# Four loads of w1 moved from SyncE's DMA queue to ScalarE's in a one-core decoder layer

## What is computed

```python
def _L0_attn_ref(x, w1, w2, b2, sparse_mask):
    attn = jnp.einsum('ds,td->st', w1, w2) * sparse_mask
    y = jnp.einsum('bds,st->bdt', x, attn) + b2
    return jax.nn.gelu(y, approximate=False)
...
x = _layernorm(x + _L0_attn_ref(x, L0_attn_w1, L0_attn_w2, L0_attn_b2, L0_attn_sparse_mask), axis=-1)
x = _layernorm(x + _L0_xattn_ref(x, ctx_4096, ctx_4096, mask_BxSxS2_ff0, ...), axis=-1)
x = _layernorm(x + _L0_ffn_ref(x, ...), axis=-1)
```

## Time and profile before

| | |
|---|---|
| median of 3 runs | 491.17 us |
| the profiled execution, its time | 490.72 us |
| its span, first to last instruction | 488.9 us |
| TensorE busy | 474.7 us (97%) |
| VectorE busy | 409.8 us (84%) |
| ScalarE busy | 269.2 us (55%) |
| GpSimd busy | 253.7 us (52%) |
| mean granted TensorE clock | 0.989 |

### The profile page before, as it was taken

One profiled execution on the slowest core, in us unless ns is written; L12 is line 12 of the kernel. 1 busy time (PEld: TensorE's weight loads), 2 busy tenths in 40 slices (PEclk: granted clock), 3 DMA queues, 4 the chain that ended last, 5 costly groups with the idle time before them and its releaser, 6 DMA issues.

```text
span 488.9 us, 11036 instructions
## 1 busy us (share of the span) xinstructions
PE 474.7 (97%) x4189; PEld 395.6 (81%) x4189; DVE 409.8 (84%) x733; ACT 269.2 (55%) x475; POOL 253.7 (52%) x250
## 2 busy tenths in 40 slices
PE   8999999999999999999999999999999999969994
PEld 8888778888888888888888888888888888757783
DVE  2779898988987898799879987998798989989666
ACT  4574447734673567356636673566357445574434
POOL 3377537863674477546746663677268421222300
PEclk9999999999999999999999999999999999979998
DMA  8942300230023002301130203021102300000004
GB/s 277 351 148 88 129 1 1 87 131 1 2 86 129 0 7 79 129 0 38 48 129 0 85 6 124 0 86 44 41 0 87 56 12 2 1 0 1 0 3 172
DMA packets 29137, 31.56 MB, mean 65 GB/s; under 512 B 6321, under 2 KB 16817, under 8 KB 29114
## 3 DMA queue, kind: packets, MB, share of 16 engines
q1 hardware_dynamic: 29114, 31.25, 19.5%
HBM read 29.15 MB, written 2.10 MB: 64 GB/s over the span
## 4 chain that ended last, share of the span: by engine, by line
PE 83%; DVE 12%; POOL 2%; ACT 1%; issue 1%; POOLq 0%; DVEq 0%; ACTq 0%
PE bank L262 24%; PE bank L264 23%; PE bank L263 23%; PE bank L370 7%; PE bank L394 3%; DVE VWl L1152 2%; DVE X L1252 1%; DVE BST L1200 1%; PE bank L283 1%; PE bank L268 1%; DVE X L1343 1%; DVE XTl L1152 1%; DVE QR L1186 1%; DVE bank L1280 1%; PE bank L427 0%
## 5 line engine op out<-in xcount | busy, mean ns | idle before, releaser
L1745 POOL TENSOR_TENSOR QS<-QS,SIN 128x512 f32<-128x512 f32 x64 | 82.9, 1295 | 132.3 <-ACT QS L802 132.3
L262 PE MATMUL bank<-XTh,WQh 128*128 128x512 f32 x256 | 102.0, 398 | 0.5 <-DVE XTl L1152 0.5
L264 PE MATMUL bank<-XTh,WQl 128*128 128x512 f32 x256 | 100.0, 391 | 0.0
L263 PE MATMUL bank<-XTl,WQh 128*128 128x512 f32 x256 | 99.7, 390 | 0.0
L1152 DVE TENSOR_TENSOR VWl<-bank,VWh 64x512 fp32r<-64x512 f32 x128 | 88.1, 688 | 9.7 <-ACT VWh L802 8.0
L802 ACT ACTIVATE QS<-bank 128x512 f32<-128x512 f32 x64 | 38.3, 598 | 96.9 <-PE bank L264 96.4
L802 ACT ACTIVATE VWh<-bank 64x512 fp32r<-64x512 f32 x128 | 75.7, 592 | 20.2 <-PE bank L264 17.5
L1280 DVE TENSOR_TENSOR bank<-bank,COS 128x512 f32<-128x512 f32 x64 | 44.6, 697 | 20.9 <-ACT QS L802 20.4
L262 PEld LDWEIGHTS bank<-XTh,WQh 128*128 128x128 f32 x256 | 48.1, 188 | 11.2 <-issue 1.2
L264 PEld LDWEIGHTS bank<-XTh,WQl 128*128 128x128 f32 x256 | 48.0, 188 | 10.5
L263 PEld LDWEIGHTS bank<-XTl,WQh 128*128 128x128 f32 x256 | 48.2, 188 | 9.4
(11 more groups left out here) (155 smaller groups left out, 954.5 us busy)
## 6 DMA issues: line engine op xcount, KB each, us to landing
WQr<-in_L_xattn_wq_dram SPq DMA_DIRECT2D x8, 1024.0 KB, 5.5
WOr<-in_L_xattn_wo_dram SPq DMA_DIRECT2D x8, 1024.0 KB, 5.1
KVr<-in_L_xattn_wk_dram SPq DMA_DIRECT2D x8, 256.0 KB, 5.1
KVr<-in_L_xattn_wv_dram SPq DMA_DIRECT2D x8, 256.0 KB, 5.4
out_dram<-X SPq DMA_DIRECT2D x8, 256.0 KB, 2.0
X<-in_x_dram SPq DMA_DIRECT2D x3, 512.0 KB, 10.1
WQr<-in_L_attn_w_dram SPq DMA_DIRECT2D x4, 256.0 KB, 5.1
WOr<-in_L_attn_w_dram SPq DMA_DIRECT2D x4, 256.0 KB, 5.3
```

Of the source, the lines that this page charges most:

```text
L262: pe.matmul(o, lh, rh, start=start, stop=False)
L263: pe.matmul(o, lh, rl, start=False, stop=False)
L264: return pe.matmul(o, ll, rh, start=False, stop=stop)
L1745: pool.tensor_tensor(q, q, SIN[:, :].unsqueeze(1).broadcast_to([P, 2, S]), ALU.mult)\
```

## The change

SyncE's program loses the four loads of w1. They now stand at the head of ScalarE's program, ahead of `w1_hi(0)`, and so are issued on ScalarE's own DMA queue. Sources, targets, sizes and semaphores are as before.

```diff
@@ SyncE
             for c in range(C):
                 sp.dma_start(WQr[:, :, c * P:(c + 1) * P], rows(w2)[:, :, c * P:(c + 1) * P]).then_inc(w2_in[c], 16)
-                sp.dma_start(WOr[:, c, :], rows(w1)[:, c, :]).then_inc(w1_in[c], 16)
             for i in range(2):
                 sp.dma_start(X[:, i, :], x_v[:, i, :]).then_inc(x_in[i], 16)
@@ ScalarE
+            for c in range(C):
+                act.dma_start(WOr[:, c, :], rows(w1)[:, c, :]).then_inc(w1_in[c], 16)
             w1_hi(0)
             w2_hi(0)
             w2_hi(1)
```

## The result

The changed kernel takes 493.38 us (median of 15 runs, 491.65 to 494.0), against 491.28 us for the kernel before (15 runs, 489.85 to 492.3): a ratio of 1.0037, 95% interval 1.0028 to 1.0046. It is slower by 2.1 us by the medians, by 1.9 us by the means. The profiled execution took 493.78 us with a span of 492.0, 3.1 us above the one of before.

The account below looks back on a forecast made before the run. The prediction took TensorE to bound the kernel, busy 474.7 of 488.9 us. Its terms, SyncE 0, ScalarE 0, TensorE's gap after clock +2.2, wq 0, gave 491.17 + 2.2 = 493.4 us; own range 492.3 to 494.5, over all cases 491.2 to 494.6.

Parts of the forecast that it names:

- SyncE and ScalarE, 0 and 0: Load issues at the start: four fewer on SyncE gain 0, four more on ScalarE at 0.50 us each cost 0.
- slow issues: Rival, ScalarE's start: an issue takes over 0.9 us, TensorE waits for VectorE, +1.6 us, 492.8; chance 0.07.
- Fine turns: The forecast, DMA engines at the start: runs alternate between queues, w2 chunk 0 lands at 6.3 us, 492.3 to 494.5; chance 0.48.
- coarse turns: Rival, same place: one or two w1 chunks precede w2 chunk 0, gap 0.6 to 1.2 us, +0.3 to +0.9; chance 0.24.
- begins at the same instant: DMA queues at the start: w1's data on its own queue begin together with those of w2 chunk 0, about 1.8 us.
- one run from each queue in turn: DMA engines at the start: alternating runs put all four w1 chunks ahead, so w2 chunk 0 lands 2.7 us later.
- What a gap costs: TensorE before the first products: a 2.6 us gap plus its effect on the faster pace costs 1.1 to 3.3, taken as 2.2 us.
- Nothing later gives it back: After 18.96 us: the start's delay stays, all rows after 20 us shifted by one and the same amount.
- Faster: Rival, work behind SyncE's removed issues: comes about 1 us earlier, gains some 0.3 us by the rows; 490.1 or less, chance 0.05.
- hidden: Rival, loads at the start: w2 chunk 0 isn't delayed and nothing is late, 491.0 to 491.3; chance 0.13.

Follow-up runs that it names:

- e1: Changed kernel with ScalarE's four loads of w1 held back by 0.76 us, until GpSimd's identity is done: 491.52 us, ratio 1.001.
- e3: Changed kernel with two identity matmuls moved from behind w2_transpose(0) to ahead of it (7 and 5 instead of 5 and 7): 491.19 us, ratio 1.0002.
- e7: Kernel before, one queue, with w2_transpose(0) also waiting for ScalarE's first copy of w1, so TensorE idles 0.9 us: 493.08 us, ratio 1.0047.
- e8: Changed kernel run once more, unaltered, for a second profile: 493.59 us.
- e2: Changed kernel with the queues exchanged, w2 on ScalarE's and w1 on SyncE's: 493.85 us, ratio 1.0063.
- e5: Changed kernel with all of w1 as one load of 1 MB on ScalarE's queue: 494.11 us, ratio 1.0072.
- e10: Changed kernel with ScalarE's loads of w1 held back only until GpSimd's first instruction is done, about 0.25 us: 491.37 us, ratio 1.0013.
- e6: Changed kernel with w2 chunk 0 as four loads of 64 KB (128 runs each) instead of one of 256 KB: 494.62 us, ratio 1.0086.
- e4: Kernel before, with 3 instead of 5 identity matmuls ahead of w2_transpose(0) and no load moved: 491.81 us, ratio 1.0015.
- e9: Changed kernel with w1 chunk 0 on SyncE behind w2 chunk 0, ScalarE's other w1 loads held back, second identity group 4 instead of 7: 492.28 us, ratio 1.0031.

## Why the prediction was right, and which of its steps was not

The forecast was slower by 2.2 us, 493.4; measured is 2.1 us, 493.38. The mechanism is shown in its outline: w2 chunk 0 has the least slack, the loads of w1 delay it (e1), and TensorE's gap is the loss (e3 and e7). But the sum came out by two errors that cancel, and it deserves no credit for its closeness.

**SyncE and ScalarE, 0 and 0: right.** ScalarE takes 0.47 us for an issue, 0.50 was assumed, and "slow issues" falls. Issuing x and the rest earlier gained nothing (e3: no gap, same time as before).

**When each queue has packets, and how an engine divides itself between them: the first wrong, the second near.** Fine turns were forecast, with all four chunks of w1 ahead of w2 chunk 0, landing at 6.3 us, and a gap of 2.6. Measured: landing at 4.7 us and a gap of 0.8. That is the number of the rival "coarse turns" (4.3 to 5.0), but not its mechanism: that one or two chunks of w1 go ahead as a whole is the rival's assumption, and no run shows it. One chunk of w1 is 0.67 us of transfer, by the rate of 389 GB/s, and the delay was 1.1 us.

The step that failed is "begins at the same instant". The forecast had both loads ready at 1.8 us and all of w1 ready behind. In fact w2 chunk 0 has its first packet near 2.9 us (2.6 in e8), and w1 chunk 1 near 3.9, though issued at 1.2. In every profile with two loads of 256 KB or more issued within 0.25 us of each other, the second one's packets appear 0.7 to 1.1 us behind the first one's, whichever queue it is on and whichever load it is (w2 second: the changed kernel, e2, e3, e8; w1 second: e5, e10). Where both queues had packets they went about one for one in most of the windows read, as "fine turns" has it: between 512 runs and 512 (e5, 123 to 126), and also between a chunk of 128 runs and one of 512 (44 to 41 in the changed kernel, 58 to 69 in e10, 71 to 82 in e1). Not in all: 78 of w1 to 24 of w2 in e6 (3.4 to 3.9 us), 44 to 231 in e10 (3.7 to 4.2 us). What was missing was w1's packets and not the turns. Why a load's packets appear late, and why the chunk of 128 runs is first when both are issued at once, stays open.

That an engine takes one run from each queue in turn was the forecast's assumption. The trace doesn't tell the 16 engines apart, so the nearly equal numbers here fit turns of one run and turns of several alike.

**What a gap costs: under-sized.** For coarse turns the forecast took a gap of 0.6 to 1.2 us of which half comes back, +0.3 to +0.9. The gap was 0.8 us and cost 2.35. By the two chains, after less before: TensorE resumes 0.82 later and its transposes take 0.24 more; 14 matmuls +0.47; four transposes +0.41; two products +0.37; together 2.31 us. More than half of the loss is the slow pace going on until 10.4 instead of 6.9 us. The forecast had this effect, but priced it for the large gap alone, and read the rise before at 6.6 us where the rows give 6.9. Its 0.113 us for a matmul at the faster pace is shown (rows 7, and 0.44 us for four transposes in rows 3), and so is 0.213 at the slower (0.85 us for four). That a gap in itself does this is shown by e4 (0.55 us idle, nothing later at its end, pace 1.5 us later) and e7.

**Nothing later gives it back: right.** +2.35 at 21 us is +2.34 at 433 us. What was not foreseen is the second slow stretch near 430 us, where the shift grows further: by 0.6 us in the profiled pair.

**Faster, hidden:** neither came. w2 chunk 0 was delayed, and no wait behind the loads turned into a gain.

## What to carry to other kernels

Before a load is put on a second queue, look at the load with the least slack and at what would share the DMA engines with it: of two loads of 256 KB issued at once, the packets of one appeared 0.7 to 1.1 us behind the other's in the profiles here, and while both had packets the one with runs of 512 bytes got the smaller share of the bytes (in the changed kernel 0.02 of 0.11 MB from 2.9 to 3.2 us). A lead of 0.76 us for the urgent load removed the loss here, one of 0.23 us in most executions only. TensorE is kept busy with fillers here until its pace rises, and an idle gap among them cost more than itself: 0.55 us made the first product 0.69 us later (e4), and 0.8 us made the first mask product 2.35 us later. In this kernel the fillers have to reach to the latest landing, and moving two of them (e3, ratio 1.0002) made it indifferent to the change. The second queue saved SyncE's issue time; since the chain shows TensorE alone, that bought nothing here (e3).

## What the runs showed that I had not expected

The pace rises at very different moments, for the same TensorE program. Busy without a gap from 1.52 us, it rose near 6.9 us (before) and 5.3 us (e1), worked out from the spacing as above. After a gap it rose near 8.4 us (resumed at 3.71, e4), 9.9 (4.92, e7), 10.3 and 10.4 (4.86 and 4.84, the two profiles of the changed kernel), 10.0 (6.15, e5: 14 matmuls in 2.86 us from 7.23). From resuming to the rise that is 3.8 to 5.6 us. Each microsecond of it is worth half a microsecond of time (1 - 0.113 / 0.213 = 0.47), so these 1.8 us are 0.9 us of time, against a spread of 2.4 us between executions of the kernel before (489.85 to 492.3 us). It can be a part of the spread; that wasn't tested. Another part goes with the later slow stretches, by the mean granted clock of each execution, which doesn't contain the first one: of the 63 executions of the kernel before that were run beside the experiments, the 10 at 0.995 have a median of 490.07 us, and the 32 at 0.989 one of 491.32.

The granted clock is shown as 1.00 in the whole first slow stretch, while the identity matmuls are spaced 0.213 us there and 0.113 us later. In the second, near 430 us, and in e9 it reads 0.50 with the same spacing. At the start of an execution of this kernel the spacing has to be read and not the clock.
